# Scan weights split at other experts, the last group's loads in another order, and routed rows turned by VectorE from two buffers

## What is computed

```python
xn = layernorm(x)
x = x + L0_attn(xn) + L0_ffn(xn)     # chunked attention; 16 experts (256 -> 128 -> 256), all of them on every row
xn = layernorm(x)
x = x + L1_attn(xn) + L1_ffn(xn)     # 4 linear scans, the top 2 mixed; 8 experts (256 -> 1024 -> 256), one per row
```

## Time and profile before

| | before |
|---|---|
| median of 3 runs | 1040.9 us (1040.36 to 1041.03) |
| the profiled execution | 1038.94 us, of which its span 1037.1 us |
| granted PE clock, mean | 0.998 |
| PE busy | 1023.9 us (99%) |
| DVE, ACT, POOL busy | 76%, 60%, 31% |
| stage A | 0 to about 512 us (group 6 from 381, group 7 from 444) |
| stage B | about 512 to 653 us |
| stage C | about 653 to 891 us |
| stage D | about 891 to 1037 us |

### The profile page before, as it was taken

How to read it: one execution, slowest core, us unless ns; L and a number is a source line. 1 busy time by engine, 2 the same in 40 slices (tenths; PEclk the granted TensorE clock), 3 DMA queues, 4 the chain that set the end, 5 groups by cost and what they waited for, 6 DMA issues and landing times. The chain is left out here.

```text
span 1037.1 us, 20069 instructions
## 1 busy us (share of the span) xinstructions
PE 1023.9 (99%) x6510; PEld 917.3 (88%) x6510; DVE 785.0 (76%) x1284; ACT 627.0 (60%) x1186; POOL 320.5 (31%) x284
## 2 busy tenths in 40 slices
PE   8999999999999999998999999999999999999998
PEld 7998989888898998887877888999999999888887
DVE  6876767667586777858779998876777777588887
ACT  4553445435354454544566666888888888566665
POOL 3343444444444444333542871000000000382000
PEclk9999999999999999999999999999999999999999
DMA  6236313222141322532446384587888776652203
GB/s 192 64 95 211 97 40 81 81 61 61 52 99 51 81 82 73 171 111 72 168 162 261 103 287 180 192 280 246 280 275 262 257 257 203 225 163 84 89 13 102
DMA packets 144114, 152.13 MB, mean 147 GB/s; under 512 B 69184, under 2 KB 114112, under 8 KB 143040
## 3 DMA queue, kind: packets, MB, share of 16 engines
q1 hardware_dynamic: 135296, 137.47, 41.4%
q0 software_dynamic: 3072, 8.39, 2.4%
q10 hardware_dynamic: 5696, 5.64, 1.7%
HBM read 109.20 MB, written 42.27 MB: 146 GB/s over the span
## 5 line engine op out<-in xcount | busy, mean ns | idle before, releaser
L806 POOL TENSOR_TENSOR acc<-acc,ytmp 128x512 f32<-128x512 f32 x120 | 158.1, 1317 | 250.2 <-ACT ytmp L897 230.5
L1637 ACT ACTIVATE act_o<-ps,scan_bias 128x512 f32<-128x512 f32 x189 | 129.8, 688 | 100.0 <-PE ps L393 95.8
L897 ACT ACTIVATE ytmp<-ps,sel 128x256 f32<-128x256 f32 x256 | 107.3, 470 | 100.3 <-PE ps L1175 100.0
L974 DVE SCALAR_TENSOR_TENSOR hT_l<-ps,hT_h 128x512 fp32r<-128x512 f32 (+1 forms) x136 | 88.3, 654 | 99.8 <-ACT hT_h L857 99.6
L1173 PE MATMUL ps<-vals_h,hT_h 128*128 128x256 f32 x512 | 145.6, 284 | 5.3 <-DVE hT_l L974 5.3
L1174 PE MATMUL ps<-vals_l,hT_h 128*128 128x256 f32 x512 | 144.4, 282 | 0.0
L1175 PE MATMUL ps<-vals_h,hT_l 128*128 128x256 f32 x512 | 144.1, 281 | 0.0
L857 ACT ACTIVATE hT_h<-ps 128x512 fp32r<-128x512 f32 x128 | 76.3, 596 | 88.5 <-PE ps L393 83.9
L1961 DVE TENSOR_TENSOR_SCAN h_b<-a_b,hstate,xs_b 128x512 f32<-128x512 f32 x63 | 88.0, 1396 | 30.4 <-ACT a_b L1644 27.1
L1173 PEld LDWEIGHTS ps<-vals_h,hT_h 128*128 128x128 f32 x512 | 96.9, 189 | 12.0 <-DVE hT_l L974 6.1
L1789 POOL DMA_INDIRECT late_y<-y_d,pos_i x20 | 23.1, 1154 | 272.3 <-DMA y_d<-y_sb 266.5
(11 more groups left out here) (261 smaller groups left out, 2769.9 us busy)
## 6 DMA issues: line engine op xcount, KB each, us to landing
raw<-w SPq DMA_DIRECT2D x78, 512.0 KB, 4.5
x1T<-xT_d SPq DMA_DIRECT2D x16, 512.0 KB, 5.3
comb_b<-comb_d SPq DMA_DIRECT2D x8, 1024.0 KB, 8.1
xn_d<-xn SPq DMA_DIRECT2D x15, 512.0 KB, 3.0
w_small<-w SPq DMA_DIRECT2D x14, 512.0 KB, 4.5
xs_d<-zeros ACTq DMA_DIRECT2D x1, 4992.0 KB, 19.8
x_d<-x SPq DMA_DIRECT2D x8, 512.0 KB, 4.2
xT_d<-nT_h SPq DMA_DIRECT2D x8, 512.0 KB, 2.7
```

The costliest lines, as they stand in the source:

```text
L806: pool.tensor_tensor(dst[:, 2:4, :], acc[:, 2:4, :], ytmp[:, k % 2, :, :], ALU.add).then_inc(acc23, 1)
L897: act.activation(ytmp[:, k % 2, j - 2, :], yb(k, j), ACT.Copy, scale=sel[:, j, k:k + 1]).then_inc(y_23, 1)
L974: dve.scalar_tensor_tensor(out=hT_l[:, k % 2, t], in0=ps[:, k % 2, t], scalar=0.0, in1=hT_h[:, k % 2, t].bitcast(F32), op0=ALU.max, op1=AL ...
L1637: act.activation(act_o[:, i % 2, w, :], ps[:, 3 * (i % 2) + w, :], func, bias=scan_bias[:, w, i:i + 1]).then_inc(act_g, 1)
```

## The change

Three things:

1. `LATE_SPLITS` and `LAST_SPLITS` name other experts.
2. On SP, the loads of b11 and b12 move behind `body(7)`; b00, b01, b02 and b10 stay ahead of it. The loads of l4 and l5 are untouched.
3. Stage C no longer turns rows on the PE. GpSimd loads them in quarters of 32 partitions, 256-byte pieces, into two buffers (`rows[:, 0]` for the first big slot of a round, `rows[:, 1]` for the others); one DVE instruction (`turn_rows`) turns them in 32x32 blocks, which the layout of the load and of `w1` in DRAM makes sufficient. A small slot's rows go straight to `sT_small`, so that ACT's copy of them is gone. Around slot 0 the splits of its weights come earlier, and the loads of the small slot's weights stand one place later on SP. The ranking of the last mixture moves from behind a slot into it.

```diff
-        LATE_SPLITS = {1: ["l0"], 3: ["l1"], 6: ["l2"], 7: ["l3"], 10: ["l4"], 11: ["l5"]}
-        LAST_SPLITS = {1: ["b00"], 3: ["b01"], 6: ["b02"], 7: ["b10"], 10: ["b11"], 11: ["b12"]}
+        LATE_SPLITS = {0: ["l0"], 1: ["l1"], 2: ["l2", "l3"], 4: ["l4"], 11: ["l5"]}
+        LAST_SPLITS = {0: ["b00"], 1: ["b01"], 2: ["b02", "b10"], 5: ["b11"], 6: ["b12"]}
...
-            for name in order[n_l:n_b]:
+            for name in order[n_l:n_l + N_STAGE]:
                 weight(name)
             body(GROUPS - 1, False, True)
+            for name in order[n_l + N_STAGE:n_b]:
+                weight(name)
...
             def slot(r, k):          # PE
-                pe.wait_ge(sT_ok, n + 1)
+                if small(k):
+                    pe.wait_ge(turned, n + 1)
+                else:
+                    pe.wait_ge(sT_ok, bigs(r, k) + 1)
...
-                if left(r, k) > 0:
-                    rows_T(r, k + 1)
...
             def rows_hi(r, k):       # ACT
+                act.wait_ge(turned, ROUND * r + k + 1)
+                act.activation(sT_h[:], sT32[:], ACT.Copy).then_inc(sT_hi, 1)
...
                 for q in range(FJ // 2):          # ACT, slot
                     relu(n, k, q, st * P)
                     round_e(n, q, st * P)
-                    if zero(n) and q == 1:
-                        w2_half(n, 1)
+                    if q == 1 and small(k):
+                        rows_hi(r, k + 1)
...
+            def load_rows(r, k):     # GpSimd
+                (h, _), (b, st) = rows_at(r, k), blocks(r, k)
+                n_q = P // Q32
+                for q in range(n_q):
+                    quarter = slice(q * Q32, (q + 1) * Q32)
+                    pool.dma_start(rows[quarter, h, 0:st * n_q, :],
+                                   xs_q[q][:, bass.ds(b * n_q, st * n_q), :]).then_inc(rows_in[h], 16)
+            def load_behind(r, k):
+                ahead = 3 if k == 0 else 1 if k == 1 else 2
+                if left(r, k) >= ahead:
+                    wait_alone(pool, turned, ROUND * r + k + 1)
+                    load_rows(r, k + ahead)
...
+            def turn_rows(r, k):     # DVE
+                n, (_, st) = ROUND * r + k, blocks(r, k)
+                h, filled = rows_at(r, k)
+                dve.wait_ge(rows_in[h], 16 * (P // Q32) * filled)
+                dst = sT_small if small(k) else sT32
+                if not small(k) and not zero(n):
+                    dve.wait_ge(sT_ok, bigs(r, k))
+                dve.transpose(dst[:].rearrange("p c (g r) -> p g c r", r=Q32),
+                              rows[:, h, 0:st * P // Q32, :].rearrange("p g (c a) -> p g c a", c=DC)).then_inc(turned, 1)
...
+            def low_halves(r, k):    # DVE, every slot but the first
+                n, (_, st) = ROUND * r + k, blocks(r, k)
+                for q in range(FJ // 2):
+                    low_e(n, q, st * P)
+                    if left(r, k) == 1:
+                        mixture_rank(dve, link, mix2, q)
+                    if q == (0 if small(k) else 2) and left(r, k) > 0:
+                        turn_rows(r, k + 1)
+                    if q == 2 and small(k) and left(r, k) > 0:
+                        rows_lo(r, k + 1)
+                    if q == 1 and not small(k) and bigs_left(r, k) > 0:
+                        w1_half(bigs(r, k) + 1, 0)
```

More of the change, by code:

```diff
@@ L51 @@
 CHUNK = 32
+Q32 = 32
 Q32 = 32
@@ L194, in build @@
     raw2 = rc("raw2", [P, FJ, D], F32)
-    rows = rc("rows", [P, ST, D], F32)
+    rows = rc("rows", [P, 2, ST * P // Q32, DC * Q32], F32)
     sT_h = rc("sT_h", [P, DC, SLOT], F32R)
@@ L1544, in body @@
                         to_rows(g - 1)
[L1545 to L1558, removed]
             def slot(r, k):
@@ L1684, in round_e @@
                 act.wait_ge(t_ok, FJ * n + 2 * (q + 1))
-                if zero(n) and q == 0:
-                    act.wait_ge(scan_ok, MC * B_FIRST)
+                if zero(n):
+                    act.wait_ge((xs_ok, a_ok, scan_ok, scan_ok)[q], MC * B_FIRST)
                 j = slice(2 * q, 2 * q + 2)
@@ L1701, in slot @@
                 if left(r, k) > 0:
-                    rows_hi(r, k + 1)
+                    if not small(k) and not small(k + 1):
+                        rows_hi(r, k + 1)
                     if not small(k) and bigs_left(r, k) > 0:
@@ L1965, in step, with weigh @@
                     dve.tensor_copy(hstate[:, i:i + 1], h_b[:, i % 2, GT - 1:GT]).then_inc(hst_v, 1)
+                if (g, i) != (B_FIRST - 1, MC - 1) or not isinstance(g, int):
+                    weigh(g, i)
+            def weigh(g, i):
+                n = MC * g + i
+                m, c = divmod(i, DC)
                 if i == 0:
@@ L2035, in rows_out, with first_halves @@
                                   ALU.add).then_inc(ys_ok, 1)
[L2037 to L2044, removed]
+            def first_halves():
+                low_e(0, 0, SLOT)
+                weigh(B_FIRST - 1, MC - 1)
+                low_e(0, 1, SLOT)
+                w2_half(0, 1)
+                low_e(0, 2, SLOT)
+                turn_rows(0, 1)
+                low_e(0, 3, SLOT)
+                w1_half(1, 0)
+            def low_halves(r, k):
[10 more added lines that the diff above has]
+                        w1_half(bigs(r, k) + 1, 0)
             def slot(r, k):
@@ L2051, in slot @@
                     w2_half(n, 1)
[L2052 to L2057, removed]
+                if zero(n):
+                    first_halves()
+                else:
+                    low_halves(r, k)
                 if left(r, k) > 0:
-                    if not small(k + 1):
+                    if not small(k) and not small(k + 1):
                         rows_lo(r, k + 1)
@@ L2133 @@
         "expert_bias": c(i["L1_ffn_expert_bias"]),
-        "w1": c(i["L1_ffn_w1"].reshape(E1, DC, P, 2, F1 // 2).transpose(0, 3, 2, 1, 4)),
+        "w1": c(i["L1_ffn_w1"].reshape(E1, P // Q32, DC, Q32, 2, F1 // 2).transpose(0, 4, 1, 3, 2, 5)
+                .reshape(E1, 2, P, DC, F1 // 2)),
         "b1": c(i["L1_ffn_b1"].reshape(E1, FJ, P).transpose(0, 2, 1)),
```

69 lines of the change are left out of this document (33 added, 36 removed).

## The result

The changed kernel takes 1056.8 us (median of 4 runs, 1055.9 to 1057.4) against 1040.6 us for the kernel before; the ratio is 1.0157, with a 95% interval of 1.0144 to 1.0171. It is slower by 16.2 us. The profiled execution has a span of 1055.5 us and a time of 1057.1.

A forecast was written before the change was run, and what follows sets the result against it. The PE, busy 1023.9 of 1037.1 us, was taken as the bound. Stage A +16.2 and stage C -4.6 gave +11.6 on 1038.9: 1050.5 us profiled, 1052.5 as median, range 1046 to 1057.

The forecast's parts named there:

- the sign of stage C: Stage C was forecast to get shorter: -8.6 - 1.3 + 5.3 = -4.6 us.
- Group 6, the stall: Stage A, expert 4: ACT waits 12.9 us for l4, loaded behind `body(6)`; the PE stalls 10.0 us.
- The old wait in group 6: Stage A: the wait for `hT_l` goes as l2 and l3 move and DVE catches up after the stop: -1.4 us.
- The clock: Stage A: after each of the two long stops the PE restarts at half clock, costing 2.2 us a stop.
- Group 7: Stage A: 8.8 us stall on b11 at expert 5, plus 2.2 clock, minus 5.6 for the old stall: +5.4 us.
- Stage A as a whole: Sum of groups 6 (+10.8 us) and 7 (+5.4 us): +16.2 us.
- The 78 transposes: Stage C: row transposes leave a PE without idle time, 0.11 us each: -8.6 us.
- The first slots: Start of stage C: three PE waits for `eT_l` go with the earlier splits of w1 and w2: -1.3 us.
- The small slots: Stage C: `rows_hi` between quarters delays ACT, idling the PE 0.75 us in each of seven small slots: +5.3 us.
- w1_small's place on SP: Stage C: no term for the moved load; only a clause that the DMAs' bytes stay the same.
- The rows' loads: Stage C: rows loaded by GpSimd in 256-byte pieces, costed at nothing; the 512-byte rule was quoted but not priced.
- Rival 2: Stage C: GpSimd's row loads come late, seven rounds cost +14 us, about 1066 us in all; chance 0.05.

The follow-up runs named there:

- a_landed: Kernel before with l0 to l3 and b00 to b10 split at experts 0 to 2, l4 and b11 at 10, l5 and b12 at 11, loads unmoved: 1036.2 us.
- best1: Changed kernel with a_landed's tables, all b loads ahead of `body(7)`, and the edits of c_w1s and c_w1s_hi: 1031.3 us, ratio 0.9911 to the kernel before.
- a_order: a_alone with all b loads ahead of `body(7)` again, so the new split tables alone: 1046.7 us, ratio 1.0070.
- a_alone: Kernel before with the change's two split tables and its order on SP, nothing of stage C: 1055.2 us, ratio 1.0142.
- a_ahead: Kernel before with the new split tables, but all l loads ahead of `body(6)` and all b loads ahead of `body(7)`: ratio 0.9978, stage A 511.7 us.
- c_w1s: c_alone with w1_small's loads put back between the loads of b2 and b1, where they stood before: 1036.9 us, ratio 0.9968.
- b_noT: Kernel before with one PE transpose of rows per slot, 78 become 23 (routed tokens wrong): ratio 0.9988, steady round 29.74 us instead of 30.37.
- c_alone: Changed kernel with the old split tables and the old place of all b loads, so stage C's part alone: 1041.1 us, ratio 1.0010.
- c_w1s_hi: c_w1s with `rows_hi` and `rows_lo` behind the loop over quarters in the small slot too: 1034.6 us, ratio 0.9952.
- c_w1s_whole: c_w1s with each slot's rows loaded by one DMA in 1 KB pieces instead of four in 256-byte pieces (rows in wrong order): 1036.3 us.

## Why the prediction was right or wrong

The time, 1056.8, lies within the range (1046 to 1057), near its upper end and 4.3 us above the forecast. The sign and the mechanism of both long stalls were right; the sign of stage C was wrong. The time would have missed the range but for luck: against the forecast, stage A came 1.5 us shorter and stage C 9.0 longer, and the median stood 0.3 us below the profiled time, where I had carried over 2.0 above it.

**Group 6, the stall: right.** 12.9 us of waiting on ACT were forecast and 12.4 measured; the PE's stall was 9.3 instead of 10.0, mostly because l4 landed in 3.4 us instead of 3.8.

**The old wait in group 6: half the reason.** I had it made by l2 and l3. It comes from the quarter reads through `sig_g` and `oT_h`, and the split of l3 adds 0.64 us to that chain: with the new tables 1.6 us are left in a_landed, where the reads landed late, and 0.6 in best1. The changed kernel has no such wait, and there the stop of 9.3 us had given DVE time; so the term of -1.4 was right rather by the second half of my sentence than by the first.

**The clock: the size is scatter.** I took 2.2 us a stop. In group 6, the time that the PE loses beyond the stall itself is 1.3 us in the changed kernel, 1.5 in a_order and 2.5 in a_alone, at the same place after the same stop. In group 7 of the changed kernel it is 2.4. (Worked out from the starts of the matmuls there against their spacing at full clock, 0.23 us for 512 columns and 0.12 for 256.)

**Group 7: right in sum, by three errors that offset each other.** The stall was 6.7 us, not 8.8: the quarter reads took 4.06 us to issue instead of 5.13, and b11 landed in 2.9 us, not 3.8. Against this came a stop that I did not see, 1.5 us before 510.65, which stands also in a_alone, a_order, a_landed, best1, a_ahead and c_w1s. There DVE has the last piece of the ranking and `oT_l` ahead of `relu_lo`. I had written that the slow restart gives the chain through `sig_g` and the ranking cover; the chain's second piece comes after the clock is back. Stage A as a whole: +14.7 instead of +16.2.

**The 78 transposes: mis-sized.** The term of -8.6 supposed that each lay on the path. b_noT shows 0.09 us for each in steady rounds, and nothing at the start and the end of stage C. The five steady rounds with ten transposes each give 4.5 us. In the changed kernel, whose splits come earlier, the start did gain: 2.7 us to the first small slot, of which the three waits are 1.3. What the transposes were worth there was not separated.

**The first slots: right, as long as w1_small's loads stand late.** In the changed kernel and in c_alone the three waits of 1.3 us are gone, and the PE has no other before the first small slot. With these loads back in their old place, in c_w1s and c_w1s_hi, another, of 1.0 and 0.8 us, stands in the second slot. In c_w1s ACT had waited 2.0 us for a half of w1 shortly before it; that this is its cause was not tested.

**The small slots: right.** 0.75 us was forecast for each; in the changed kernel the longest wait of each is 0.52 to 0.88 us, in c_w1s it is 0.52, or 0.69 with the restart, in six of the seven, and taking `rows_hi` from between the quarters takes it away. As said above, the time follows by less than the sum of the waits.

**w1_small's place on SP: the step that failed.** The prediction has one clause on SP's side of stage C, that the DMAs' bytes are the same, and none on what stands behind the moved 1 MB. It is 3.4 to 4.9 us of the 9.0 by which stage C was missed. The order of the queue showed it in advance: behind the new place comes the second half of w2, for which ACT asks first thing in the next slot.

**The rows' loads: no lateness, but a price elsewhere.** Rival 2 is refuted: GpSimd issued each load in 0.58 us (median of 92; 551 to 677 ns), and DVE has no wait for rows among its waits of stage C. (The time that I gave this rival does not follow from its own count: if 2.4 us a load makes 24 us a round, 4 us makes 40, which is 10 us more than a round has and not 2.) What the loads cost lies in ACT's waits for w2, 1.0 to 2.5 us if it is more than scatter. The Trainium skill ("DMA: Bandwidth & Descriptors", Specifications) wants 512 bytes a piece for full rate. The traces agree at most in direction: a w2 half lands in 5.4 us (c_w1s) and 4.9 (c_w1s_hi) beside pieces of 256 bytes, and in 4.8 (c_w1s_whole) beside 1 KB. I had quoted it and left it out of the sum for want of a row. The other rule, that a 128x128 transpose belongs on TensorE (the Trainium skill, "VectorE: DVE Perf Modes", Rules for kernel authors), did not decide: DVE took 0.70 us for the big transposition, the length I had taken, and in c_w1s_hi steady rounds are 0.75 us shorter than before, since DVE is not the bound.

A round was forecast at 30.0 us; the changed kernel's were 34.4, 31.7, 31.8 and then 30.8 to 30.5. **What stays open:** why the first rounds suffer most, and how much of the 1.7 us by which the changed kernel's stage C exceeds c_alone's is more than the scatter that c_alone itself shows.

## What to carry to other kernels

A split, a load and the body between them are one thing: neither the new table nor the new order makes the long stop in group 7 by itself, and together they cost some 8 us. For each instruction that waits on a DMA, look up where that DMA stands in its issuing queue and what stands ahead of it. When a load is moved to make room, ask at once who is first to use what is now behind it: 1 MB moved one place later cost about what the whole rewrite of stage C could win (4.2 us against the 4.1 by which c_w1s_hi's stage C is shorter than before). And what an instruction on the busiest engine is worth must be counted in the steady state first; at the ends of a stage other waits can take its place, as in b_noT.

## What the runs showed of the hardware that I had not expected

The PE's clock did not answer the same stop in the same way. In c_w1s and in c_w1s_whole the PE waits 3.62 us before 488.3 to 488.6, in the same program up to there; the first keeps its clock, the second is at half of it. Windows of 488 to 490 and 490 to 492 us, c_w1s first:

```profile
488.00:490.00 2.00, 1.45 (x12) 1.00 0.00 0
490.00:492.00 2.00, 2.00 (x13) 1.00 0.00 0
...
488.00:490.00 2.00, 1.72 (x8) 0.50 0.00 0
490.00:492.00 2.00, 2.00 (x9) 0.50 0.00 0
```

Matmul for matmul, the second falls 2.4 us behind the first within 6 us of the restart; but the first then met the ranking's stop of 1.5 us, which the second did not. Counted from the restart, the two ended 0.7 us apart. Some of the run-to-run spread of this kernel, 1 to 2 us, may come from such places; that was not tested.
